# A vit tower's top-k search on 16-bit remainders, its rank and tie counts in one turn, its MLP weights split during the stage before

## The reference

```
# tokenizer (per batch): quadratic attention without softmax, PReLU
q, k, v = x @ Wq + bq, x @ Wk + bk, x @ Wv + bv
h = prelu((d_gamma * (q @ k.T)) @ v @ Wo + bo)
# layer norm, a gated attention over channels, residual
h = h + attn(layernorm(h))
# mixture of depths: only the best half of the rows passes the MLP
n = layernorm(h)
weights = n @ wr + br                       # one number for each row
_, idx = top_k(weights, 2048); sel = idx[:2047]
y = (gelu(n[sel] @ w1 + b1) @ w2 + b2) * weights[sel]
out = h + (zeros.at[sel].set(y) + n)        # the rest passes unchanged
```

## Time and profile before

| | |
|---|---|
| three timed runs | 2093.72, 2096.09, 2096.11 us (median 2096.09) |
| profiled execution | 2093.88 us, its span 2092.2 us |
| PE busy | 1981.6 us, 95% of the span |
| DVE / ACT / POOL busy | 59% / 32% / 21% |
| mean granted clock of PE | 0.975 |
| DMA | 250 MB, 120 GB/s on average |

### The profile page before, as it was taken

The page is one execution under the profiler, slowest core; times in us unless marked ns, Lnnn a source line. Parts: engine busy times, 40 slices in busy tenths (PEclk is TensorE's granted clock), DMA queues, the critical chain, the costliest instruction groups (busy, mean ns, idle before and its releaser), DMA issues.

```text
span 2092.2 us, 27450 instructions
## 1 busy us (share of the span) xinstructions
PE 1981.6 (95%) x9540; PEld 1640.6 (78%) x9540; DVE 1237.8 (59%) x2227; ACT 674.5 (32%) x1091; POOL 440.5 (21%) x565
## 2 busy tenths in 40 slices
PE   7999999999999999999999999999999999438898
PEld 6888888888888888788888878888888788327797
DVE  4656565665656556756565565656654478756543
ACT  4422222222222226322222222222222266424454
POOL 3302020211202014302020220202012155422342
PEclk9999999999999999999999999999999999769999
DMA  4232433334343333143333424333334479310110
GB/s 141 91 101 83 156 114 121 101 120 156 94 141 111 122 119 122 61 166 116 121 111 121 149 72 161 110 121 111 111 131 171 176 278 310 124 31 21 41 42 31
DMA packets 88114, 250.14 MB, mean 120 GB/s; under 512 B 11968, under 2 KB 32448, under 8 KB 88000
## 3 DMA queue, kind: packets, MB, share of 16 engines
q1 hardware_dynamic: 84928, 240.27, 34.4%
q0 software_dynamic: 3072, 8.44, 1.3%
HBM read 194.05 MB, written 54.62 MB: 119 GB/s over the span
## 4 chain that ended last, share of the span: by engine, by line
PE 90%; DVE 5%; issue 2%; ACT 1%; DMA 1%; POOL 1%; SPq 0%; DVEq 0%; ACTq 0%; POOLq 0%
PE bank L662 34%; PE bank L677 34%; PE bank L809 4%; PE bank L1563 4%; PE bank L1583 3%; PE bank L712 3%; PE bank L1151 2%; PE bank L634 2%; PE bank L647 1%; PE bank L608 1%; PE bank L618 1%; DVE top_passed L1232 1%; DVE top_counts L1235 0%; DVE top_pivots L1229 0%; DMA prelu<-in_tok_prelu_a 0%
## 5 line engine op out<-in xcount | busy, mean ns | idle before, releaser
L677 PE MATMUL bank<-x_hi,kt 128*128 128x512 f32 x2048 | 724.2, 395 | 1.5 <-DVE work L518 1.4
L518 DVE SCALAR_TENSOR_TENSOR work<-bank,d_col,gate 128x512 f32<-128x512 f32 x512 | 383.9, 750 | 553.7 <-PE bank L677 544.4
L397 ACT ACTIVATE p_hi<-work 128x512 fp32r<-128x512 f32 x512 | 324.1, 633 | 1065.7 <-PE bank L662 1020.6
L677 PEld LDWEIGHTS bank<-x_hi,kt 128*128 128x128 f32 x2048 | 384.4, 188 | 90.7 <-DVE work L518 2.7
L662 PE MATMUL bank<-p_hi,v_hi 128*128 128x512 f32 x1024 | 407.0, 397 | 0.3 <-ACT yT L359 0.2
L662 PE MATMUL bank<-p_hi,v_lo 128*128 128x512 f32 x1024 | 404.1, 395 | 0.0
L662 PE MATMUL bank<-p_lo,v_hi 128*128 128x512 f32 x1024 | 403.4, 394 | 0.0
L677 PE MATMUL bank<-x_lo,kt 128*128 128x512 f32 x1024 | 400.9, 392 | 0.0
L506 DVE TENSOR_TENSOR p_lo<-work,p_hi 128x512 fp32r<-128x512 f32 x512 | 367.7, 718 | 29.3 <-ACT p_hi L397 29.2
L567 POOL TENSOR_SCALAR spread<-mv 128x4 f32<-128x4 f32 x16 | 5.0, 310 | 1125.6 <-DVE mv L450 1125.6
L662 PEld LDWEIGHTS bank<-p_hi,v_hi 128*128 128x128 f32 x1024 | 192.2, 188 | 50.6 <-DVE p_lo L506 5.3
(11 more groups left out here) (227 smaller groups left out, 2281.3 us busy)
## 6 DMA issues: line engine op xcount, KB each, us to landing
gate<-in_gateT SPq DMA_DIRECT2D x256, 512.0 KB, 3.6
work<-in_xT SPq DMA_DIRECT2D x32, 512.0 KB, 4.9
scratch_rows<-rows SPq DMA_DIRECT2D x16, 518.0 KB, 3.8
scratch_h<-work SPq DMA_DIRECT2D x16, 512.0 KB, 3.0
scratch_mn<-mn_sb SPq DMA_DIRECT2D x16, 512.0 KB, 6.8
scratch_mT_hi<-mT_hi SPq DMA_DIRECT2D x16, 512.0 KB, 2.7
scratch_mT_lo<-mT_lo SPq DMA_DIRECT2D x16, 512.0 KB, 4.0
gate<-scratch_mn SPq DMA_DIRECT2D x16, 512.0 KB, 4.4
```

The costliest lines, as they stand in the source:

```text
L397: nc.scalar.activation(p_hi[:, i % 2, :], p32[:, i % RP, :], ACT.Copy).then_inc(hi_done, 1)
L518: nc.vector.scalar_tensor_tensor(p32[:, i % RP, :], S[i % 2][:, :], d_col[:, i:i + 1], gate[:, g % RG, j, :], ALU.add, ALU.mult).then_inc( ...
L677: mm = pe.matmul(S[i % 2][:, :], w, x, start=n == 1, stop=n == 3 * KD)
```

## The change

Five things are changed; everything up to the mix stays.

1. **Search.** What is left to search is kept as a 16-bit unsigned remainder `left` (128x32) instead of an fp32 key and a found sum. The 15 pivots of a digit are constants then: `grid` (four digits x 15 x 32, 16-bit), made by POOL at the start of the mix. DVE counts the reached pivots and scales the digit in one instruction, subtracts it from the remainder, compares, adds up; the found sum is added behind that.
2. **Ranks and ties.** The counts of the rows above the threshold and of its ties go through PE in one turn of two matmuls (66 columns) in place of two turns with five.
3. **Lanes.** The one-hot matrices are laid out as [partition, lane, tile] instead of [partition, tile, lane], and compared with a constant `lanes` (128x4096, bf16) that POOL fills in the first four steps of the mix. The 32 matmuls read a column of each lane: every 32nd element.
4. **W1 and W2** have a buffer of their own (`ffn`); their high parts are made by ACT in mix steps 1 to 4, their low parts by POOL in steps 2 to 5, in quarters of 128x1024 or halves of each matrix.
5. **MLP.** NORM, TURN, SPLIT are 0, 4, 5; the gathers signal for each 128 rows, and normalizing and transposing wait for each by itself. Batch 1's search has its rank stage one step earlier, its 128x4096 comparison in one piece in block 3 of unit 2, and its list in block 4 of unit 2.

```diff
@@ mix, ACT: step c, half h @@
+                if 1 <= c <= len(ffn_parts):
+                    x, part = ffn_parts[c - 1]
+                    nc.scalar.activation(W3[x + "_hi"][:, part, :], mlp_raw[x][:, part, :], ACT.Copy).then_inc(pr.sem("mw_hi"), 1)
...
-            for x in ("w1", "w2"):
-                nc.scalar.activation(W3[x + "_hi"], mlp_raw[x], ACT.Copy).then_inc(pr.sem("mw_hi"), 1)
@@ mix, POOL: constants, and step c @@
+            for q in range(STEPS):
+                step = float(16 ** (STEPS - 1 - q))
+                nc.gpsimd.memset(W3["step"][:, q, :], step).then_inc(made, 1)
+                nc.gpsimd.tensor_scalar(W3["grid"][:, q], W3["index"][:, 1:PIV + 1].unsqueeze(2).to_broadcast([P, PIV, pr.ST]),
+                                        step, None, ALU.mult).then_inc(made, 1)
...
+            def spread_lanes(c):
+                few = slice(c * P // 4, (c + 1) * P // 4)
+                nc.gpsimd.tensor_copy(W3["lanes"][:, few, :], W3["index"][:, few].unsqueeze(2).to_broadcast(
+                    [P, P // 4, pr.ST])).then_inc(made, 1)
...
+                if 2 <= c <= len(ffn_parts) + 1:
+                    x, part = ffn_parts[c - 2]
+                    pool.wait_ge(pr.sem("mw_hi"), c - 1)
+                    nc.gpsimd.tensor_tensor(W3[x + "_lo"][:, part, :], mlp_raw[x][:, part, :],
+                                            W3[x + "_hi"][:, part, :].bitcast(F32), ALU.subtract).then_inc(pr.sem("mw_lo"), 1)
+                if c < 4:
+                    spread_lanes(c)
...
-            for n, x in enumerate(("w1", "w2")):
-                pool.wait_ge(pr.sem("mw_hi"), n + 1)
-                nc.gpsimd.tensor_tensor(W3[x + "_lo"], mlp_raw[x], W3[x + "_hi"].bitcast(F32),
-                                        ALU.subtract).then_inc(pr.sem("mw_lo"), 1)
@@ TopRows @@
-        self.link(v.tensor_scalar(self.pivots[:, :], self.W3["digit"][:, :], float(16 ** (STEPS - 1 - q % STEPS)),
-                                  self.found[:, 0:1], ALU.mult, ALU.add))
-        self.link(v.tensor_tensor(self.passed[:, :, :], self.key_f[:, :].unsqueeze(1).to_broadcast(shape),
-                                  self.pivots[:, :].unsqueeze(2).to_broadcast(shape), ALU.is_ge))
+        self.link(v.tensor_tensor(self.passed[:, :, :], self.left[:, :].unsqueeze(1).to_broadcast([P, PIV, self.pr.ST]),
+                                  self.W3["grid"][:, q % STEPS], ALU.is_ge))
...
-        link(v.tensor_scalar(self.reach[:, :], self.CB[:, 0:PIV], float(self.K), None, ALU.is_ge))
-        link(v.tensor_reduce(self.digit[:, :], self.reach[:, :], AX_X, ALU.add))
-        link(v.scalar_tensor_tensor(self.found[:, :], self.digit[:, :], float(16 ** (STEPS - 1 - q % STEPS)),
-                                    self.found[:, :], ALU.mult, ALU.add))
+        link(v.scalar_tensor_tensor(self.reach[:, :], self.CB[:, 0:PIV], float(self.K), self.W3["step"][:, q % STEPS, :],
+                                    ALU.is_ge, ALU.mult, accum_out=self.digit[:, 0:1]))
+        if q % STEPS < STEPS - 1:
+            link(v.tensor_scalar(self.left[:, :], self.left[:, :], self.digit[:, 0:1], 0.0, ALU.subtract, ALU.max))
+            self.dve_count(q + 1)
+        link(v.tensor_tensor(found[:, :], found[:, :], self.digit[:, :], ALU.add))
...
+        self.pr.nc.vector.tensor_tensor(self.in_lane[:, :, :], self.lane_b[:, :].unsqueeze(1).to_broadcast([P, P, self.pr.ST]),
+                                        self.W3["lanes"][:, :, :], ALU.is_equal).then_inc(self.counted, 1)
...
+            pe.matmul(self.TIES[:, 0:2 * ST + 2], before, self.of_b[:, :], start=True, stop=False)
+            mm = pe.matmul(self.TIES[:, 0:2 * ST + 2], ones, self.earlier_b[:, :], start=False, stop=True)
...
-                mm = pe.matmul(self.CB[:, 0:2 * self.Q], self.in_lane[:, t, :], self.numbers[:, t, :], start=t == 0,
+                mm = pe.matmul(self.CB[:, 0:2 * self.Q], self.in_lane[:, :, t], self.numbers[:, :, t], start=t == 0,
@@ mlp @@
-    LAG, NORM, TURN, SPLIT, HELD = 2, 1, 5, 6, 3
+    LAG, NORM, TURN, SPLIT, HELD = 2, 0, 4, 5, 3
-        x_ld = [pr.sem(f"ff_x_ld{h}") for h in range(HELD)]
+        x_ld = [[pr.sem(f"ff_x_ld{h}{j}") for j in range(TPC)] for h in range(HELD)]
...
+                act.wait_ge(x_ld[u % HELD][j], landed(u))
                 if j == 0:
-                    act.wait_ge(x_ld[u % HELD], landed(u))
...
+            def search(g):
+                n = g // 2
+                if g % 2 == 0 and n <= 2 * STEPS:
+                    top.dve_stage(1, n)
+                elif g == 4 * STEPS + 2:
+                    top.dve_places(1)
+                elif g == 4 * STEPS + 3:
+                    top.dve_lanes()
+                elif g == 4 * STEPS + 4:
                     top.dve_list(1)
...
-                    if j % 2 == 0 and 0 <= n < top.TURNS - 1:
+                    if j % 2 == 0 and 0 <= n < top.TURNS:
                         top.pe_turn(1, n)
...
-                    if u == 3 and j == 0:
-                        top.pe_turn(1, top.TURNS - 1)
```

More of the change, by code:

```diff
@@ L1187, in __init__ @@
         ST = pr.ST
-        self.Q = pr.T // 2 // P
-        (self.w_br, self.key_f, self.low_f, self.above, self.equal, self.cum, self.last, self.moved) = (
-            sbuf("top_" + n, [P, ST]) for n in ("w_br", "key", "low", "above", "equal", "cum", "last", "moved"))
-        self.sign, self.key, self.part, self.place, self.tile, self.lane = (
-            sbuf("top_" + n, [P, ST], I32) for n in ("sign", "bits", "part", "place", "tile", "lane"))
-        self.equal_b, self.earlier_b, self.pick = (sbuf("top_" + n, [P, ST], BF16) for n in ("equal_b", "earlier", "pick"))
@@ L1194, in __init__ @@
-        self.passed, self.counts = sbuf("top_passed", [P, PIV, ST], BF16), sbuf("top_counts", [P, PIV], BF16)
-        self.pivots, self.reach = sbuf("top_pivots", [P, PIV]), sbuf("top_reach", [P, PIV])
-        self.found, self.digit, self.need = (sbuf("top_" + n, [P, 1]) for n in ("found", "digit", "need"))
-        self.above_n, self.zero = sbuf("top_above_n", [P, 2], BF16), sbuf("top_zero", [P, ST])
-        self.in_lane = sbuf("top_in_lane", [P, ST, P], BF16)
-        self.in_tile, self.numbers = sbuf("top_in_tile", [P, ST, self.Q], BF16), sbuf("top_numbers", [P, ST, 2 * self.Q], BF16)
@@ L1200, in __init__ @@
-        self.low_part, self.rows = sbuf("top_low_part", [P, self.Q]), sbuf("top_rows", [P, pr.B, self.Q], I32)
+        Q = self.Q = pr.T // 2 // P
+        self.w_br, self.key_f, self.low_f, self.scaled, self.full, self.no, self.place_f = (
+            sbuf("top_" + n, [P, ST]) for n in ("w_br", "key", "low", "scaled", "full", "no", "place_f"))
+        self.sign, self.bits, self.part, self.low, self.place, self.tile, self.lane = (
+            sbuf("top_" + n, [P, ST], I32) for n in ("sign", "bits", "part", "low_bits", "place", "tile", "lane"))
@@ new lines, in __init__ @@
+        self.left = sbuf("top_left", [P, ST], U16)
+        self.passed, self.counts = sbuf("top_passed", [P, PIV, ST], BF16), sbuf("top_counts", [P, PIV], BF16)
+        self.reach = sbuf("top_reach", [P, PIV])
+        self.high_found, self.low_found, self.digit, self.n_above = (
+            sbuf("top_" + n, [P, 1]) for n in ("high_found", "low_found", "digit", "n_above"))
+        self.of, self.cum, self.rank = (sbuf("top_" + n, [P, 2, ST]) for n in ("of", "cum", "rank"))
+        self.of_b, self.earlier_b = (sbuf("top_" + n, [P, 2 * ST + 2], BF16) for n in ("of_b", "earlier"))
@@ L1201, in __init__ @@
+        self.zero = sbuf("top_zero", [P, ST])
+        self.tile_b, self.lane_b = (sbuf("top_" + n, [P, ST], BF16) for n in ("tile_b", "lane_b"))
+        self.in_lane = sbuf("top_in_lane", [P, P, ST], BF16)
+        self.numbers = sbuf("top_numbers", [P, 2 * Q, ST], BF16)
+        self.in_tile = sbuf("top_in_tile", [P, Q, ST], BF16)
+        self.low_part, self.rows = sbuf("top_low_part", [P, Q]), sbuf("top_rows", [P, pr.B, Q], I32)
         self.CB, self.TIES = pr.banks[2], pr.banks[3]
@@ L1295, in dve_places @@
[L1295 to L1304 removed]
+        link(v.tensor_copy(self.lane_b[:, :], self.lane[:, :]))
@@ L1640, in build @@
         router = sb(nc, ctx, "router", [P, batches, pr.ST])
-        W3 = {"b1": sb(nc, ctx, "b1", [P, FT]), "digit": sb(nc, ctx, "digit", [P, PIV])}
+        W3 = {"b1": sb(nc, ctx, "b1", [P, FT])}
+        W3["grid"] = sb(nc, ctx, "grid", [P, STEPS, PIV, pr.ST], U16)
+        W3["step"] = sb(nc, ctx, "step", [P, STEPS, PIV])
+        W3["lanes"] = sb(nc, ctx, "lanes", [P, P, pr.ST], BF16)
         W3["ones"], W3["before"] = sb(nc, ctx, "ones", [P, P], BF16), sb(nc, ctx, "before", [P, P], BF16)
```

194 lines of the change are left out of this document (81 added, 113 removed).

## The result

The changed kernel takes 2071.97 us in the median of four runs (2068.24 to 2072.95); the kernel before, timed beside it, 2095.40. The medians lie 23.4 us apart, and the ratio is 0.9885 with a 95% interval of 0.9871 to 0.9898: 1.15% faster. The forecast was 2071, with a range of 2060 to 2083.

| stretch | before | after | difference | forecast |
|---|---|---|---|---|
| to the first matmul of the mix behind its wait for DVE | 1666.2 | 1667.0 | +0.8 | 0 |
| from there to the first key of the search | 143.1 | 149.3 | +6.2 | +1.0 |
| first key to the list of batch 0 | 44.4 | 28.4 | -16.0 | -15.0 |
| list to the first MLP matmul | 14.1 | 11.3 | -2.8 | -3.0 |
| units 0 to 3 | 118.6 | 109.8 | -8.8 | -7.1 |

What follows compares the result with a forecast made beforehand. PE sets the pace in the mix; batch 0's search, the way to the first MLP matmul and units 0 to 3 can give time. Terms sum to -24.1 from 2093.88, 2069.8 by the profiled execution; forecast 2071, range 2060 to 2083.

Steps and rivals of the forecast that it cites:

- The stall: Batch 0's search: two DVE instructions beside POOL's split of W1 and W2 fall to their clean price, -8.4.
- the prediction's argument on DVE and POOL: Mix: a two-input DVE instruction contends with POOL reading SBUF; blocking low parts would ask 9 of DVE's 17 us.
- The search otherwise: Batch 0's search without the stall: shorter turns, keys, end and lanes, -7.4 in sum.
- 16 bits bring nothing: Rival, search and unit 2's lanes: comparisons keep their price for an element; about 2078, chance 0.12.
- The bad ends of this sum: The search otherwise at the unfavourable bounds of its terms: -2.6 in place of -7.4.
- The lane matmuls: PE's 32 matmuls reading every 32nd element: +0.8 in batch 0's search, +0.5 in unit 2.
- From the list to the MLP: Batch 0's list to first MLP matmul: three row tiles are through before the fourth gather lands, -3.0 (at worst 0).
- Units 0 to 3: First four MLP units: losses fall from 24.3 to 17.2, -7.1, despite new waits in units 0 and 2.
- Both new waits: PE waits 3.7 in unit 0 for DVE's keys beside POOL's base rows, 3.9 in unit 2 for lanes.
- The mix: Mix stage: POOL's added low parts, lanes and grid mostly fit its free time, +1.0 (bounds 0 and 5).
- the prediction's own signs: Profile after: first key within 2 us of where it stood; wrong if the mix ends 4 or more later.
- POOL holds up the mix: Rival, mix steps 0 to 5: POOL's added work delays its statistics, then DVE, ACT, PE, 29.7; about 2100, chance 0.05.

Runs made afterwards that it cites:

- `top_left` in the experiment: Changed kernel with the split of W1 and W2 made behind the mix again, in four pieces on ACT then POOL; 2078.70 us in one run.
- the repeated pivots: Changed kernel, its comparison reading each pivot of the 16-bit grid repeated 32 times in place of the spread constant; 2072.65 us in one run.
- the runs show: Changed kernel plus grid later, base rows earlier, lane turn later, one-hot tiles in runs of 8, 16, 2: 2056.00, 2054.60, 2053.16 us.
- as the experiment shows: Changed kernel, the first normalization of a unit waiting for all four gathers again; 2069.72 us in one run.
- the old NORM: Changed kernel with NORM, TURN and SPLIT at 1, 5 and 6 as before; 2077.96 us, ratio 0.9918 to the kernel before.

## Why the prediction was right, point by point

- *The stall*, -8.4: shown, by its going and by its coming back (8.9) with the split behind the mix. Of the two instructions that stood still, only the comparison reads two tensors, as the prediction's argument on DVE and POOL has it. The pivots, like `top_left` in the experiment, read one tensor and one number for each partition, and stood still as well.
- *The search otherwise*, -7.4: right, but short by 1.6; -9.0 was measured (-16.0 without the stall and the lane matmuls). A turn lost 0.56 where 0.4 were reckoned, mostly since reading the accumulator costs 0.08 in place of 0.2. The price taken for dense 16-bit operands, 0.5 ns (0.44 and 2.2), met 0.41 and 2.29. The rival that 16 bits bring nothing is right for repeated operands only, as the repeated pivots show. (The bad ends of this sum, as far as its terms give them, come to -3.1, not -2.6, which takes that rival's 2078 down by half a microsecond.)
- *The lane matmuls*, +0.8 and +0.5: too small, +1.4 at both places. The Trainium skill's page "SBUF — State Buffer", section "Door 1: The DMA port swizzle", had warned rightly of a stride of 32, but its 8 numbers free of cost are not what the runs show. At a stride of 8 the matmuls take 2.23, nearly the 2.39 of 32 and far from the 1.03 of 2. The measurement decides.
- *From the list to the MLP*, -3.0: measured -2.8, in two parts (1.6 and 1.2) that the prediction took as one. Behind unit 0 the gain isn't seen any more, as the experiment shows.
- *Units 0 to 3*, -7.1: measured -8.8. Both new waits came, 2.77 for 3.7 and 3.80 for 3.9. The cause given for the first, keys that stand beside POOL's addition, was wrong in the instruction: it was `act_lo`. The stretches at 1.2 GHz behind them were 6.8 us long each, not 3.4 as in the earlier trace rows, and cost 2.6 and 1.4 where 1.7 each were reckoned. Units 1 and 3 lost their waits as forecast. For unit 3, 34.2 before and 23.5 after, it is the earlier list and not the earlier normalization: with the old NORM it takes 23.6.
- *The mix*, +1.0: the step that failed. It measured +6.2, above the upper bound of 5, and the first key came 7.1 later by the clock. By the prediction's own signs (the first key within 2, wrong if the mix ends 4 or more later) this part is wrong. It counted the grid only as POOL's time, 3 to 5, out of 46 free. As the path to PE it named the low parts, with the statistics and the next gating behind them; it didn't see that the first gating stands behind the grid, where POOL had 1.73 free for work of 5.68. The grid alone makes it all: a wait of 3.51, then 6.83 us at 1.2 GHz, 6.1 of them with PE at work, which is 3.0 more. That is the mechanism of the rival "POOL holds up the mix", at the start of the stage and once, not in four steps. The split and lanes in the steps cost nothing that shows.
- The total came out within 1 us because this +5.2, with +0.8 ahead of the mix and +0.2 behind the list, was met by -1.0 in the search, -1.7 in units 0 to 3 and -0.4 behind them. The profiled execution still lies 3.1 above the 2069.8 reckoned for it, and the rest is made up by a median that lies 1.0 below the profiled execution and by the 1.2 added to the sum. That the forecast comes so near is luck; the direction and the stretches other than the mix are not.

## What to carry to other kernels

A constant that an otherwise idle engine makes "for free" has to be made where no other engine waits for that one: the same 5.7 us of POOL cost 3.6 to 6.3 at the start of a stage and nothing that shows in its middle. A wait of PE costs more than its length when the clock falls behind it (here 2.6 and 1.4 on top of 2.77 and 3.80), so a new wait of 3 to 4 us is worth moving. What the clock costs is counted over the work that runs at half speed, not over the whole stretch: time in which PE waits anyway, and matmuls that the clock doesn't limit, are not part of it. And where one engine writes a buffer along one axis and another reads it along the other, short runs (here pairs, in one run) can serve both at their dense price.
